# Inverse roots of the norms in the feed-forward part: ScalarE's square root against a guess and two iteration steps on VectorE

## The chip, the cores and the metric

One core of a Trainium2 chip runs one program. The metric is the device time of one execution in microseconds, the median over the runs shown. Lower is better. TensorE (PE), ScalarE (ACT), VectorE (DVE), GpSimd (POOL) and SyncE (SP) run their own instruction streams and meet through semaphores.

## The reference

One transformer layer with the norms behind the parts, on x of 2 x 2048 tokens by 256. What matters here are the three norms of each token, marked below, each with a mean, a variance and an inverse root.

```
z   = softmax(causal(q k^T / 8)) v              # 16 heads of 64
x1  = layernorm(x + z W_out + b_out)            # norm 1
h   = (x1 - mu) * rsqrt(var + 1e-5) * gamma + beta   # norm 2
u   = silu(h w1 + b1)                           # 1024 wide
out = layernorm(x1 + 0.5 * (u w2 + b2))         # norm 3
```

## The kernel before

**Attention** fills the first 1476 us and isn't touched. It leaves its outputs in DRAM, split in two float16 halves.

**Feed-forward part.** The 4096 tokens go in 8 blocks of 512 (`TOKB`, step i = 0 to 7, at most two blocks in flight), a block being 4 tiles of 128 tokens (`TPB`). Each engine has one function (`feed_forward_tensor`, `_scalar`, `_vector`, `_gpsimd`, `_sync`) and walks the steps in a fixed order, so the order of the work is the order written in these functions. Two blocks of out-projection and the first block's norms come ahead of step 0.

- PE, `step` (L1174): 11 turns of a loop over f. `fc1(i, f)` for f < 8 makes 128 of the 1024 columns (6 matmuls of 512 columns); `fc2(i, f-3)` follows three turns behind (12 matmuls of 256 columns); at f = 8 `turn(i+1)` (L1145) transposes the next block's normed rows, for which it waits on `norm_ready`. For i < 6 `out_projection(i+2)` (96 matmuls) ends the step.
- ACT, `step` (L1206): for each f a Silu out of PSUM into `a_full` (L1214) and two scaled Copies (L1218) into `a_hi` and `a_scaled`. Between them it takes the square roots of the norms, `root(n)` (L1202): the two of the next block behind f = 3 and f = 5, the one of norm 3 behind the step (that of step 6 behind f = 1 of step 7). In the trace an ACT_TABLE_LOAD stands ahead of a root that follows a Silu, and one ahead of the next Silu; `preload_silu` (L1230) takes the latter early.
- POOL (L1112): for each f one subtraction `a_lo = a_scaled - a_hi`, for which `fc2` waits (`a_split`).
- DVE, `step` (L1328): `to_norms(i+1)` (norms 1 and 2 of the next block, then `base`), `to_hT(i+1)` (scaled copies of the transposed rows out of PSUM, `hT_hi`, `hT` and `hT_lo`, for which the next step's `fc1` waits on `hT_ready`), then norm 3 of block i into `res`, which SP stores. `to_norms` starts when the block's out-projection is done (`wo_ready`).

A norm (`normalise`, L1256) is four BN_STATS, four BN_AGGR, an addition of EPS into `var_e` (L1265), a wait for ACT's root, a reciprocal (L1267) and four `tensor_scalar` (L1269) that subtract the mean and multiply by `rstd`. `Chain.done` lets each step of it raise a semaphore and waits for it on DVE itself.

Of the kernel before, what the change touches and what calls it, by code (L numbers as in the profile page):

```python
# [20 lines left out]
I32 = mybir.dt.int32  # L21
ALU = mybir.AluOpType
ACT = mybir.ActivationFunctionType
AX = mybir.AxisListType

P = 128
B, S, D = 2, 2048, 256
# [7 lines left out]
QB = 512  # L35
NQ = S // QB
NBLK = 2 * NQ
TPB = QB // P
# [3 lines left out]
START = 1  # L42
# [5 lines left out]
EPS = 1e-5  # L48
# [216 lines left out]
def program(nc, x, xT, wqkv, wout, b_out, gamma, beta, q1, s1, b1, q2, s2, b2, out, zT_dram):  # L265

    with ExitStack() as ctx:
        def sb(name, shape, dt=F32):
            return ctx.enter_context(nc.sbuf_tensor(name, shape, dt))

        def sem(name):
            return ctx.enter_context(nc.semaphore(name))
# [51 lines left out]
        def flat(t, dims, dt):  # L324
# [4 lines left out]
        w_hi_all, w_lo_all = flat(w_hi[:, :, :, :], 3, F32), flat(w_lo[:, :, :, :], 3, F32)  # L329
# [15 lines left out]
        y, ya, o = [w_hi_all[:, TPB * D * a:TPB * D * a + TPB * D].rearrange("p (t d) -> p t d", t=TPB) for a in range(3)]  # L345
        bo_s, b2_s, hb2 = [w_lo_all[:, D * a:D * a + D] for a in range(3)]
        a_scaled = w_lo_all[:, 3 * D:3 * D + 2 * QB].rearrange("p (d t) -> p d t", d=2)
        gam, bet, b1_s = sb("gam", [P, DT]), sb("bet", [P, DT]), sb("b1_s", [P, FT])
# [6 lines left out]
        res = qa_all[:, 0:SB].rearrange("p (k t d) -> p k t d", k=2, t=TPB)  # L355
# [6 lines left out]
        x1 = p_full_all[:, 4096:4096 + TPB * D].rearrange("p (t d) -> p t d", t=TPB)  # L362
        xn = p_parts_all[:, 4096:4096 + TPB * D].rearrange("p (t d) -> p t d", t=TPB)
        preload = sb("preload", [P, 1])
        stats, mv, var_e, std, rstd = (sb(n, d) for n, d in (("stats", [P, TPB, 6]), ("mv", [P, TPB, 2]),
                                                             ("var_e", [P, TPB]), ("std", [P, TPB]), ("rstd", [P, TPB])))
        WO, HT, FC, ZO = 0, 2, 4, 6

        passed = sem("passed")
# [24 lines left out]
        wo_ready, wo_read = sem("wo_ready"), sem("wo_read")  # L394
        first_norms, last_norm = sem("first_norms"), sem("last_norm")
        norm_ready, hT_ps, hT_parts, hT_ready = sem("norm_ready"), sem("hT_ps"), sem("hT_parts"), sem("hT_ready")
        var_ready, std_ready = sem("var_ready"), sem("std_ready")
        fc1_ready, act_ready, a_split = sem("fc1_ready"), sem("act_ready"), sem("a_split")
        fc2_used = sem("fc2_used")
        fc2_read = sem("fc2_read")  # L400
# [1 line left out]
        preloaded = sem("preloaded")  # L402
        silu_done, ffn_consts = sem("silu_done"), sem("ffn_consts")
        stored = [sem("stored0"), sem("stored1")]
# [3 lines left out]
        FIRST_PROJECTED = 0  # L408
        W_COLS = DF // W_PIECES
        SHIFT_ROWS = 6  # L410
        CONSTS = 13

        def reach(eng, semaphore, value):
# [129 lines left out]
        def attention_gpsimd(pool):  # L543
# [23 lines left out]
            for k, (dst, value) in enumerate(rows):  # L567
                if k:
                    pool.wait_ge(shift_rows, k)
                nc.gpsimd.memset(dst, value).then_inc(shift_rows, 1)  # L570
            pool.wait_ge(shift_rows, SHIFT_ROWS)

# [528 lines left out]
        def projects(i):  # L1101
            return FIRST_PROJECTED <= i < TOKB - 2
# [94 lines left out]
        def feed_forward_scalar(act):  # L1197
            act.sem_inc(act_ready, START)
            act.sem_inc(silu_done, START)
            act.sem_inc(preloaded, START)  # L1200

            def root(n):  # L1202
                act.wait_ge(var_ready, n + 1)
                nc.scalar.activation(std[:, :], var_e[:, :], ACT.Sqrt).then_inc(std_ready, 1)

            def step(i, k, more):  # L1206
                for f in range(FT):
                    act.wait_ge(fc1_ready, i * FT + f + 1 + START)

                    act.wait_ge(fc2_used, i * FT + START)  # L1210

                    act.wait_ge(a_split, i * FT + max(0, f - 1) + START)
                    at = i * FT + f + 1
                    nc.scalar.activation(a_full[:, f % 2, :], psum[:, FC + f % 2, :], ACT.Silu, bias=b1_s[:, f:f + 1],  # L1214
                                         scale=u_inverse[:, :]).then_inc(silu_done, 1)
                    act.wait_ge(silu_done, at + START)
                    for dst in (a_hi[:, f, :], a_scaled[:, f % 2, :]):
                        last = nc.scalar.activation(dst, a_full[:, f % 2, :], ACT.Copy, scale=a_scale[:, :])  # L1218
                    last.then_inc(act_ready, 1)
                    if f == 1 and i and not projects(i - 1):  # L1220
                        root(3 * i + 1)
                    if more and f in ROOTS_AT:
                        root(3 * i + 2 + ROOTS_AT.index(f))
                if not more:
                    root(3 * i + 2)
                elif projects(i):
                    root(3 * i + 4)
                    preload_silu(i + 1)

            def preload_silu(n):  # L1230


                act.wait_ge(preloaded, sum(projects(i) for i in range(n - 1)) + (n > 0) + START)
                nc.scalar.activation(preload[:, :], b1_s[:, 0:1], ACT.Silu).then_inc(preloaded, 1)

            ROOTS_AT = (3, 5)

            root(0)
            root(1)
            preload_silu(0)  # L1240
            over_blocks(act, step)

        def feed_forward_vector(dve):
# [9 lines left out]
                    instruction.then_inc(self.sem, 1)  # L1253
                    dve.wait_ge(self.sem, self.at)

            def normalise(chain, src, dst, n):  # L1256

                for t in range(TPB):
                    last = nc.vector.bn_stats(stats[:, t, :], src[:, t, :])
                chain.done(last)  # L1260
                dve.sem_inc(passed, 1)
                for t in range(TPB):
                    last = nc.vector.bn_aggr(mv[:, t, :], stats[:, t, :])
                chain.done(last)
                nc.vector.tensor_scalar(var_e[:, :], mv[:, :, 1], EPS, None, ALU.add).then_inc(var_ready, 1)  # L1265
                dve.wait_ge(std_ready, n + 1)
                chain.done(nc.vector.reciprocal(rstd[:, :], std[:, :]))  # L1267
                for t in range(TPB):
                    last = nc.vector.tensor_scalar(dst[:, t, :], src[:, t, :], mv[:, t, 0:1], rstd[:, t:t + 1],  # L1269
                                                   ALU.subtract, ALU.mult)  # L1270
                return last

            def constants():

# [18 lines left out]
                nc.vector.tensor_scalar(gam_s[:, :], gam[:, :], h_scale[:, :], None, ALU.mult)  # L1293
                step(nc.vector.tensor_scalar(bet_s[:, :], bet[:, :], h_scale[:, :], None, ALU.mult))

            NORMS, LAST = 9, 3

            def to_norms(i, k, n):
                chain = Chain(first_norms, i * NORMS)
                dve.wait_ge(wo_ready, i + 1)  # L1300
                dve.wait_ge(x_in[k], 16 * ((i - k) // 2 + 1) if isinstance(i, int) else (i - k) * 8 + 16)
                to = ZO if i == 1 else WO
                sums = psum[:, to:to + 2, :].rearrange("p k (t d) -> p (k t) d", t=2)
                b = i // NQ
                nc.vector.scalar_tensor_tensor(out=y[:, :, :], in0=sums, scalar=z_power[:, b:b + 1], in1=xs[:, k, :, :],
                                               op0=ALU.mult, op1=ALU.add).then_inc(wo_read, 1)
                dve.wait_ge(wo_read, i + 1 + START)
                chain.done(nc.vector.tensor_tensor(ya[:, :, :], y[:, :, :], bo_s.unsqueeze(1).to_broadcast([P, TPB, D]), ALU.add))
                chain.done(normalise(chain, ya, x1, n))

                last = normalise(chain, x1, xn, n + 1)
                last.then_inc(norm_ready, 1)
                nc.vector.scalar_tensor_tensor(out=base[:, k, :, :], in0=x1[:, :, :], scalar=2.0,
                                               in1=hb2.unsqueeze(1).to_broadcast([P, TPB, D]),
                                               op0=ALU.mult, op1=ALU.add).then_inc(first_norms, 1)
# [11 lines left out]

            def step(i, k, more):  # L1328
                if more:
                    to_norms(i + 1, 1 - k, 3 * i + 2)  # L1330
                    to_hT(i + 1)
                chain = Chain(last_norm, i * LAST)
                dve.wait_ge(fc2_used, i * FT + FT + START)
                dve.wait_ge(first_norms, i * NORMS + NORMS)

                dve.wait_ge(res_ready, i + START)
                sums = psum[:, ZO:ZO + 2, :].rearrange("p k (t d) -> p (k t) d", t=2)
                nc.vector.scalar_tensor_tensor(out=o[:, :, :], in0=sums, scalar=o_inverse[:, :], in1=base[:, k, :, :],
                                               op0=ALU.mult, op1=ALU.add).then_inc(fc2_read, 1)
                dve.wait_ge(fc2_read, i + 1 + START)  # L1340

                dve.wait_ge(stored[k], (((i - k) // 2) * 16 if isinstance(i, int) else (i - k) * 8) + START)
                last = normalise(chain, o, res[:, k, :, :], 3 * i + 4 if more else 3 * i + 2)
                last.then_inc(res_ready, 1)

            dve.wait_ge(biases_in, 16 * 2)
            nc.vector.tensor_scalar(hb2, b2_s, 0.5, None, ALU.mult).then_inc(b2_halved, 1)
            dve.wait_ge(b2_halved, 1)
            constants()
            to_norms(0, 0, 0)  # L1350
            to_hT(0)
            over_blocks(dve, step)

# [63 lines left out]
```

## Time and profile before

| | us |
|---|---|
| median of 3 runs (lowest to highest) | 1784.78 (1783.34 to 1786.6) |
| the profiled execution, its own time | 1787.09 |
| span of the profiled execution | 1785.2 |
| feed-forward part, from the first out-projection (1476.2) to the end | 309.0 |
| busy share of the span: PE, DVE, ACT, POOL | 95%, 78%, 88%, 76% |

How to read it: busy shares are of the whole span, most of which is attention. "Idle before" is the time an engine stood still ahead of an instruction, with the instruction that released it. Times of the trace are microseconds from the start of the span.

### The profile page before, as it was taken

How to read it: one execution, taken by the hardware profiler on the slowest of the kernel's cores; microseconds unless marked ns; L12 is line 12 of the kernel's file. 1: busy time of each engine (PE TensorE's matmuls, PEld its weight loads, DVE VectorE, ACT ScalarE, POOL GpSimd, SP SyncE). 2: the span in 40 equal slices, each digit the busy share in tenths (PEclk: the TensorE clock that was granted, in tenths of full speed). 3: DMA queues.
4: the chain of work that ended last, by engine and by line, in shares of the span. 5: the costliest groups of instructions: out<-in, count | busy, mean ns of one | idle time of the engine just before them, and what ended most of it. 6: DMA issues, size and time to landing. Idle time of an engine off the chain costs nothing.

```text
span 1785.2 us, 53985 instructions
## 1 busy us (share of the span) xinstructions
PE 1690.5 (95%) x21839; PEld 1152.2 (65%) x21839; DVE 1384.4 (78%) x3200; ACT 1562.2 (88%) x3243; POOL 1352.6 (76%) x833
## 2 busy tenths in 40 slices
PE   4799999999999999999999999999999998889986
PEld 2466666666666666666666666666666656666664
DVE  7978798978787878797989897989796845565554
ACT  4599999999999999999998999999999993765676
POOL 3498989898989898989898989888989891222223
PEclk9899999999999999999999999999999999999999
DMA  4003121211111111151212111111111502222300
GB/s 136 13 20 102 22 52 24 51 26 49 25 50 24 50 25 50 26 167 26 49 26 49 26 49 25 49 26 49 26 50 26 172 14 89 71 72 94 120 12 24
DMA packets 113207, 91.82 MB, mean 51 GB/s; under 512 B 73152, under 2 KB 100032, under 8 KB 111808
## 3 DMA queue, kind: packets, MB, share of 16 engines
q1 hardware_dynamic: 112960, 88.38, 18.3%
q8 instruction: 173, 2.83, 0.7%
q14 instruction: 74, 0.61, 0.1%
HBM read 33.82 MB, written 20.97 MB: 31 GB/s over the span
## 4 chain that ended last, share of the span: by engine, by line
PE 65%; ACT 21%; POOL 5%; DVE 4%; issue 4%; DMA 1%; SPq 0%; DVEq 0%; ACTq 0%
PE psum L1010 10%; PE psum L980 10%; PE psum L1014 10%; PE psum L951 7%; PE psum L1127 6%; PE psum L1038 5%; PE psum L1036 5%; PE psum L1040 5%; ACT p_parts L682 5%; ACT p_full L683 5%; PE psum L965 4%; POOL p_parts L578 4%; ACT kb L1214 2%; ACT w_lo L1218 2%; ACT p_full L1218 1%
## 5 line engine op out<-in xcount | busy, mean ns | idle before, releaser
L578 POOL TENSOR_TENSOR p_parts<-p_full,p_parts 128x1024 f16<-128x1024 f32 (+1 forms) x640 | 1161.1, 1841 | 196.4 <-ACT p_full L683 194.4
L682 ACT ACTIVATE p_parts<-psum 128x512 f16<-128x512 f32 (+3 forms) x1280 | 731.0, 571 | 60.6 <-PE psum L1014 35.2
L683 ACT ACTIVATE p_full<-psum 128x512 f32<-128x512 f32 (+3 forms) x1280 | 738.6, 579 | 0.0
L749 DVE TENSOR_REDUCE row_max<-psum 128x1 f32<-128x512 f32 x768 | 484.2, 681 | 16.1 <-PE psum L980 12.7
L1036 PE MATMUL psum<-v,p_parts 128*128 128x65 f16 x4352 | 487.2, 193 | 7.7 <-POOL p_parts L578 4.7
L1038 PE MATMUL psum<-v,p_parts 128*128 128x64 f16 x4352 | 488.7, 194 | 0.0
L1040 PE MATMUL psum<-v,p_parts 128*128 128x65 f16 x4352 | 486.2, 192 | 0.0
L1036 PEld LDWEIGHTS psum<-v,p_parts 128*128 128x128 f16 x4352 | 406.6, 97 | 83.7 <-POOL p_parts L578 12.5
L1010 PE MATMUL psum<-qa,ka 128*128 128x512 f16 (+3 forms) x1280 | 444.0, 348 | 4.0 <-ACT p_full L683 3.5
L1038 PEld LDWEIGHTS psum<-v,p_parts 128*128 128x128 f16 x4352 | 402.7, 97 | 69.6
L1014 PE MATMUL psum<-qb,kb 128*128 128x512 f16 (+3 forms) x1280 | 443.8, 347 | 3.0 <-DVE qb L762 2.9
L1040 PEld LDWEIGHTS psum<-v,p_parts 128*128 128x128 f16 x4352 | 404.2, 99 | 0.0
L980 PE MATMUL psum<-ka,qa 128*128 128x512 f16 (+3 forms) x1280 | 382.3, 347 | 11.0 <-DMA ka<-ka 2.4
L746 DVE CUSTOM_DVE_ANT_0 psum<-psum,mask_q 128x128 f32<-128x128 f32 (+3 forms) x512 | 238.2, 515 | 13.1 <-PE psum L980 11.3
L1118 POOL TENSOR_TENSOR p_parts<-w_lo,p_full 128x512 f16<-128x512 f32 x64 | 73.9, 1155 | 222.3 <-ACT w_lo L1218 222.3
L1010 PEld LDWEIGHTS psum<-qa,ka 128*128 128x128 f16 x1280 | 124.6, 97 | 75.9 <-ACT p_full L683 26.8
L1014 PEld LDWEIGHTS psum<-qb,kb 128*128 128x128 f16 x1280 | 124.9, 98 | 68.3 <-DVE qb L762 5.3
L980 PEld LDWEIGHTS psum<-ka,qa 128*128 128x128 f16 x1280 | 113.7, 97 | 80.7 <-DVE row_max L749 3.9
L775 DVE SCALAR_TENSOR_TENSOR qa<-psum,q_scale,qa 64x512 f16<-64x512 f32 x128 | 95.9, 749 | 67.8 <-ACT qa L668 66.8
L780 DVE TENSOR_TENSOR kb<-psum,ka 64x512 f16<-64x512 f32 x128 | 87.6, 684 | 46.6 <-ACT ka L671 45.7
L1016 PE MATMUL psum<-mask_k,ident_b 128*128 128x128 bf16 x512 | 111.6, 220 | 0.0
L1127 PE MATMUL psum<-ka,x_lo 128*128 128x512 f16 x384 | 93.1, 387 | 16.1 <-ACT kb L1214 11.7
(143 smaller groups left out, 2507.2 us busy)
## 6 DMA issues: line engine op xcount, KB each, us to landing
zT_dram<-z_T SPq DMA_DIRECT2D x16, 1024.0 KB, 4.7
qb<-qa SPq DMA_DIRECT2D x128, 64.0 KB, 1.9
ka<-ka SPq DMA_DIRECT2D x128, 64.0 KB, 1.9
shared_z<-zT_dram SPq DMA_DIRECT2D x4, 2048.0 KB, 8.4
x_hi<-zT_dram SPq DMA_DIRECT2D x4, 2048.0 KB, 9.4
shared_z<-xT_dram SPq DMA_DIRECT2D x8, 512.0 KB, 7.5
x_lo<-x_dram SPq DMA_DIRECT2D x8, 512.0 KB, 10.0
out_dram<-qa SPq DMA_DIRECT2D x8, 512.0 KB, 3.3
```

The lines of the kernel that those rows point to most:

```text
L578: nc.gpsimd.tensor_tensor(p_lo[:, at % NP, cols], p_full[:, at % NP, cols], p_hi[:, at % NP, cols], ALU.subtract).then_inc(probs_split, 1)
L682: nc.scalar.activation(p_hi[:, at % NP, to], lane_bank(a)[:, P * f:QB], ACT.Exp, scale=1.0 / SCORE)
L683: nc.scalar.activation(p_full[:, at % NP, to], lane_bank(a)[:, P * f:QB], ACT.Exp, scale=1.0 / SCORE).then_inc(lane_read, 1)
L746: nc.vector.tensor_tensor_reduce(out=bank, in0=bank, in1=mask_q[:, QB - w:QB], scale=1.0, scalar=NEG, op0=ALU.add, op1=ALU.max, accum_out= ...
L749: nc.vector.reduce_max(most, bank, AX.X).then_inc(ring_read, 1)
L980: last = nc.tensor.matmul(bank[:, 0:w], qa[:, h, P * tile:P * tile + P], ka[:, h, QB * c:QB * c + w], start=True, stop=True)
L1010: nc.tensor.matmul(to, ka[:, h, keys], qa[:, h, cols], start=True, stop=False)
L1014: last = nc.tensor.matmul(to, kb[:, h, keys], qb[:, h, cols], start=False, stop=k < TPB * q)
L1036: nc.tensor.matmul(z, p_hi[:, at % NP, cols], v[:, m % 2, k, h, 0:VZ], start=(k == 0 and t == 0), stop=False, skip_group_check=True)
L1038: nc.tensor.matmul(z[:, 0:C], p_hi[:, at % NP, cols], v[:, m % 2, k, h, V_LO:VS], start=False, stop=False, skip_group_check=True)
L1040: done = nc.tensor.matmul(z, p_lo[:, at % NP, cols], v[:, m % 2, k, h, 0:VZ], start=False, stop=last, skip_group_check=True)
L1127: mm = nc.tensor.matmul(psum_out, stationary[a], moving[b], start=first and n == 0, stop=last and n == 2, skip_group_check=True)
```

## The change

In the feed-forward part ACT takes no roots: `root` and its calls, the semaphores `var_ready` and `std_ready` and the repeated `preload_silu` go; one Silu at the start loads the table. DVE keeps the statistics and forms the inverse root in eight instructions on 128x4 elements, each chained to the one before by a semaphore: a guess out of the bits of `var_e` (one `tensor_scalar` on integers) and two iteration steps (`tensor_tensor` and `scalar_tensor_tensor`). One `dve.sem_inc(passed, 1)` behind BN_STATS goes as well. The small tiles lie in unused columns of `w_lo_all`, and norm 3 gets a mean and a root of its own. Nothing of the attention part, of PE, POOL and SP is changed.

```diff
-        stats, mv, var_e, std, rstd = (sb(n, d) for n, d in (("stats", [P, TPB, 6]), ("mv", [P, TPB, 2]),
-                                                             ("var_e", [P, TPB]), ("std", [P, TPB]), ("rstd", [P, TPB])))
+        small = w_lo_all[:, 3 * D + 2 * QB:3 * D + 2 * QB + 18 * TPB]
+        stats = small[:, 0:6 * TPB].rearrange("p (t s) -> p t s", t=TPB)
+        mvs = [small[:, (6 + 2 * a) * TPB:(8 + 2 * a) * TPB].rearrange("p (t s) -> p t s", t=TPB) for a in range(2)]
+        var_e, guess, near, part, ratio, bend = [small[:, a * TPB:a * TPB + TPB] for a in range(10, 16)]
+        rstds = [small[:, a * TPB:a * TPB + TPB] for a in range(16, 18)]
...
-            def root(n):
-                act.wait_ge(var_ready, n + 1)
-                nc.scalar.activation(std[:, :], var_e[:, :], ACT.Sqrt).then_inc(std_ready, 1)
...
-                    if f == 1 and i and not projects(i - 1):
-                        root(3 * i + 1)
-                    if more and f in ROOTS_AT:
-                        root(3 * i + 2 + ROOTS_AT.index(f))
-                if not more:
-                    root(3 * i + 2)
-                elif projects(i):
-                    root(3 * i + 4)
-                    preload_silu(i + 1)
...
-            root(0)
-            root(1)
-            preload_silu(0)
+            nc.scalar.activation(preload[:, :], b1_s[:, 0:1], ACT.Silu).then_inc(preloaded, 1)
+            act.wait_ge(preloaded, 1)
...
-            def normalise(chain, src, dst, n):
+            def spread(chain, src, mv, rstd):
                 for t in range(TPB):
                     last = nc.vector.bn_stats(stats[:, t, :], src[:, t, :])
                 chain.done(last)
-                dve.sem_inc(passed, 1)
                 for t in range(TPB):
                     last = nc.vector.bn_aggr(mv[:, t, :], stats[:, t, :])
                 chain.done(last)
-                nc.vector.tensor_scalar(var_e[:, :], mv[:, :, 1], EPS, None, ALU.add).then_inc(var_ready, 1)
-                dve.wait_ge(std_ready, n + 1)
-                chain.done(nc.vector.reciprocal(rstd[:, :], std[:, :]))
+                chain.done(nc.vector.tensor_scalar(var_e[:, :], mv[:, :, 1], EPS, None, ALU.add))
+                inverse_root(chain, var_e, rstd)
+
+            def inverse_root(chain, of, root):
+                chain.done(nc.vector.tensor_scalar(guess[:, :].bitcast(I32), of[:, :].bitcast(I32), -0.5, GUESS_BITS, ALU.mult, ALU.add))
+                chain.done(nc.vector.tensor_tensor(part[:, :], guess[:, :], of[:, :], ALU.mult))
+                chain.done(nc.vector.tensor_tensor(ratio[:, :], part[:, :], guess[:, :], ALU.mult))
+                chain.done(nc.vector.scalar_tensor_tensor(out=bend[:, :], in0=ratio[:, :], scalar=-10.0 / 3.0, in1=ratio[:, :],
+                                                          op0=ALU.add, op1=ALU.mult))
+                chain.done(nc.vector.scalar_tensor_tensor(out=near[:, :], in0=bend[:, :], scalar=5.0, in1=guess[:, :],
+                                                          op0=ALU.add, op1=ALU.mult))
+                chain.done(nc.vector.tensor_tensor(part[:, :], near[:, :], of[:, :], ALU.mult))
+                chain.done(nc.vector.scalar_tensor_tensor(out=ratio[:, :], in0=part[:, :], scalar=-0.5 * 0.375 ** 3, in1=near[:, :],
+                                                          op0=ALU.mult, op1=ALU.mult))
+                chain.done(nc.vector.scalar_tensor_tensor(out=root[:, :], in0=ratio[:, :], scalar=1.5 * 0.375, in1=near[:, :],
+                                                          op0=ALU.add, op1=ALU.mult))
```

## Rows read from the trace of the kernel before

**Rows 1.** Waits, 1470 to 1786 us: who waited for whom; us in total, times, longest

```profile
PE psum L1127 <- ACT kb L1214: 11.7, 15, 2.2
...
PE psum L1127 <- POOL p_parts L1118: 8.6, 14, 0.7
...
PE psum L1150 <- DVE p_parts L1269: 8.5, 8, 1.2
```

**Rows 2.** Timeline of PE, step 6: start us, us, instruction, count [idle before <-releaser]

```profile
1726.11 4.05 PE L1127 MATMUL psum<-ka,x_lo 128*128 128x512 f16 x18
...
1730.48 1.47 PE L1127 MATMUL psum<-ka,x_lo 128*128 128x512 f16 x6 [0.32 <-ACT kb L1214]
...
1731.79 0.38 PE L1127 MATMUL psum<-w_raw_rest,p_full 128*128 128x256 f16 x2
...
1733.10 1.46 PE L1127 MATMUL psum<-ka,x_lo 128*128 128x512 f16 x6
...
1739.54 1.47 PE L1127 MATMUL psum<-ka,x_lo 128*128 128x512 f16 x6 [1.07 <-ACT kb L1214]
...
1746.09 1.09 PE L1150 MATMUL psum<-ident,p_parts 128*128 128x128 f32 x8 [1.17 <-DVE p_parts L1269]
...
1747.02 0.38 PE L1127 MATMUL psum<-w_raw_rest,p_full 128*128 128x256 f16 x2
...
1752.53 4.05 PE L1127 MATMUL psum<-ka,x_lo 128*128 128x512 f16 x18
```

**Rows 3.** Timeline of step 2, ScalarE, GpSimd and VectorE

```profile
1580.01 0.78 ACT L1214 ACTIVATE kb<-psum,b_s,u_inverse 128x512 f32<-128x512 f32 x1 [6.57 <-PE psum L1127]
...
1582.06 0.76 ACT L1214 ACTIVATE kb<-psum,b_s,u_inverse 128x512 f32<-128x512 f32 x1
...
1582.23 1.16 POOL L1118 TENSOR_TENSOR p_parts<-w_lo,p_full 128x512 f16<-128x512 f32 x1 [15.58 <-ACT w_lo L1218]
...
1583.25 0.17 DVE L1265 TENSOR_SCALAR var_e<-mv 128x4 f32<-128x4 f32 x1
...
1591.11 0.78 ACT L1214 ACTIVATE kb<-psum,b_s,u_inverse 128x512 f32<-128x512 f32 x1
```

**Rows 4.** Timeline of PE: starts of step 0, step 2 and the wait in step 7

```profile
1503.07 7.74 PE L1127 MATMUL psum<-ka,x_lo 128*128 128x512 f16 x24 [4.36 <-issue]
...
1510.64 0.38 PE L1127 MATMUL psum<-w_raw_rest,p_full 128*128 128x256 f16 x2
...
1578.51 4.05 PE L1127 MATMUL psum<-ka,x_lo 128*128 128x512 f16 x18
...
1761.88 1.47 PE L1127 MATMUL psum<-ka,x_lo 128*128 128x512 f16 x6 [2.20 <-ACT kb L1214]
```

**Rows 5.** Timeline of VectorE: to_hT's subtraction ahead of step 0; copies and subtraction in step 6

```profile
1501.74 1.23 DVE L1326 TENSOR_TENSOR ka<-kb,ka 128x1024 f16<-128x1024 f32 x1
...
1747.23 1.53 DVE L1322 TENSOR_SCALAR ka<-psum,gam_s,bet_s 128x512 f16<-128x512 f32 x2
...
1750.23 2.00 DVE L1326 TENSOR_TENSOR ka<-kb,ka 128x1024 f16<-128x1024 f32 x1
```

**Rows 6.** Timeline of VectorE: the last norm, at the end

```profile
1777.76 1.40 DVE L1259 BATCH_NORM_STATS2 stats<-w_hi 128x6 f32<-128x256 f32 x4
...
1779.72 0.17 DVE L1265 TENSOR_SCALAR var_e<-mv 128x4 f32<-128x4 f32 x1
...
1780.38 1.38 DVE L1269 TENSOR_SCALAR qa<-w_hi,mv,rstd 128x256 f32<-128x256 f32 x4
```

**Rows 7.** Timelines of GpSimd and VectorE: two places where they meet

```profile
1477.25 1.15 POOL L584 TENSOR_TENSOR z_parts<-z_pair,z_parts 128x512 f16<-128x512 f32 x1 [2.16 <-ACT z_parts L690]
...
1477.68 0.73 DVE L1287 SCALAR_TENSOR_TENSOR a_bound<-u_inverse,a_bound 128x1 f32<-128x1 f32 x1
...
1593.34 1.16 POOL L1118 TENSOR_TENSOR p_parts<-w_lo,p_full 128x512 f16<-128x512 f32 x1 [3.83 <-ACT w_lo L1218]
...
1593.42 1.10 DVE L1265 TENSOR_SCALAR var_e<-mv 128x4 f32<-128x4 f32 x1
```

More of the change, by code:

```diff
@@ L396, in program @@
         norm_ready, hT_ps, hT_parts, hT_ready = sem("norm_ready"), sem("hT_ps"), sem("hT_parts"), sem("hT_ready")
-        var_ready, std_ready = sem("var_ready"), sem("std_ready")
         fc1_ready, act_ready, a_split = sem("fc1_ready"), sem("act_ready"), sem("a_split")
@@ L410, in program @@
         SHIFT_ROWS = 6
+        GUESS_BITS = float(0x5f3759df)
         CONSTS = 13
@@ L1199, in feed_forward_scalar @@
             act.sem_inc(silu_done, START)
-            act.sem_inc(preloaded, START)
-            def root(n):
-                act.wait_ge(var_ready, n + 1)
-                nc.scalar.activation(std[:, :], var_e[:, :], ACT.Sqrt).then_inc(std_ready, 1)
             def step(i, k, more):
@@ L1219, in step @@
                     last.then_inc(act_ready, 1)
-                    if f == 1 and i and not projects(i - 1):
-                        root(3 * i + 1)
-                    if more and f in ROOTS_AT:
-                        root(3 * i + 2 + ROOTS_AT.index(f))
-                if not more:
-                    root(3 * i + 2)
-                elif projects(i):
-                    root(3 * i + 4)
-                    preload_silu(i + 1)
[L1230 to L1236, printed above, removed]
-            root(0)
-            root(1)
-            preload_silu(0)
+            nc.scalar.activation(preload[:, :], b1_s[:, 0:1], ACT.Silu).then_inc(preloaded, 1)
+            act.wait_ge(preloaded, 1)
             over_blocks(act, step)
@@ L1264, in normalise, with rescale @@
                 chain.done(last)
-                nc.vector.tensor_scalar(var_e[:, :], mv[:, :, 1], EPS, None, ALU.add).then_inc(var_ready, 1)
-                dve.wait_ge(std_ready, n + 1)
-                chain.done(nc.vector.reciprocal(rstd[:, :], std[:, :]))
+                chain.done(nc.vector.tensor_scalar(var_e[:, :], mv[:, :, 1], EPS, None, ALU.add))
[13 more added lines that the diff above has]
+                                                          op0=ALU.add, op1=ALU.mult))
+            def rescale(src, dst, mv, rstd):
                 for t in range(TPB):
@@ L1271, in normalise @@
                 return last
+            def normalise(chain, src, dst):
+                spread(chain, src, mvs[0], rstds[0])
+                return rescale(src, dst, mvs[0], rstds[0])
             def constants():
@@ L1294, in constants, with to_norms @@
                 step(nc.vector.tensor_scalar(bet_s[:, :], bet[:, :], h_scale[:, :], None, ALU.mult))
-            NORMS, LAST = 9, 3
-            def to_norms(i, k, n):
+            SPREAD = 11
+            NORMS, LAST = 2 * SPREAD + 3, SPREAD
+            def to_norms(i, k):
                 chain = Chain(first_norms, i * NORMS)
@@ L1308, in to_norms @@
                 chain.done(nc.vector.tensor_tensor(ya[:, :, :], y[:, :, :], bo_s.unsqueeze(1).to_broadcast([P, TPB, D]), ALU.add))
-                chain.done(normalise(chain, ya, x1, n))
-                last = normalise(chain, x1, xn, n + 1)
+                chain.done(normalise(chain, ya, x1))
+                last = normalise(chain, x1, xn)
                 last.then_inc(norm_ready, 1)
@@ L1329, in step @@
                 if more:
-                    to_norms(i + 1, 1 - k, 3 * i + 2)
+                    to_norms(i + 1, 1 - k)
                     to_hT(i + 1)
@@ L1340, in step @@
                 dve.wait_ge(fc2_read, i + 1 + START)
-                dve.wait_ge(stored[k], (((i - k) // 2) * 16 if isinstance(i, int) else (i - k) * 8) + START)
-                last = normalise(chain, o, res[:, k, :, :], 3 * i + 4 if more else 3 * i + 2)
+                dve.wait_ge(stored[k], ((i - k) // 2) * 16 + START)
+                spread(chain, o, mvs[1], rstds[1])
+                last = rescale(o, res[:, k, :, :], mvs[1], rstds[1])
                 last.then_inc(res_ready, 1)
@@ L1349, in feed_forward_vector @@
             constants()
-            to_norms(0, 0, 0)
+            to_norms(0, 0)
             to_hT(0)
```

## The prediction

> **What bounds the kernel now.** The change touches nothing ahead of 1476 us, so I read the waits of the feed-forward part alone, then the timeline of PE through one block, then what ScalarE, GpSimd and VectorE did beside it.
>
> VectorE's own waits for ScalarE's roots cost nothing as long as nobody waits for VectorE, so the waits to read are PE's [rows 1]: 11.7 us for Silu, 8.6 us for GpSimd's subtraction, 8.5 us for VectorE's normed rows.
>
> The timeline of one block [rows 2] gives PE's prices. One fc1 issues in 1.31 us (1730.48 to 1731.79), one fc2 in 1.31 (to 1733.10), a pair in about 2.61 when nothing is late (several pairs; the one shown takes 2.62), the turn in 0.93 (1746.09 to 1747.02). The start, from the first fc1 to the first fc2, takes 5.68 (1726.11 to 1731.79). Against these prices PE loses in the block:
> - 1739.54 - (1733.10 + 2 x 2.61) = 1.22 ahead of an fc1, for Silu;
> - 1746.09 - (1739.54 + 2 x 2.61) = 1.33 ahead of the turn, for the norms;
> - 1752.53 - 1747.02 - 3 x 1.31 = 1.58 between the last fc2s, for GpSimd, which is late because ScalarE is.
>
> Sum 4.13 us. All of it hangs on ScalarE. Its cadence for one f is 2.05 us [rows 3], less than PE's 2.61, so without roots ScalarE is never last. But the Silu due at 1582.06 + 3 x 2.04 = 1588.18 starts at 1591.11: a root with a table load ahead and one behind puts it 2.93 us back, twice in a block. The block's period is (1726.11 - 1578.51) / 4 = 36.90 [rows 2, 4]; the floor by PE's own work is 36.90 - 4.13 = 32.77.
>
> **The change, part by part.**
>
> *ScalarE without roots, steps 1 to 5:* the three losses go, 5 x 4.13 = 20.65 us, if nothing else is late. GpSimd's first subtraction ends at 1582.23 + 1.16, 4.88 after the step's start of 1578.51 [rows 3, 4]; it is wanted at 5.68, and later ones are earlier still against their fc2.
>
> *Step 0* starts at 1503.07 and takes 7.57 to its first fc2 (1510.64) [rows 4], slower than the 5.68 elsewhere; I keep that. Before, it lasted to 1578.51 - 36.90 = 1541.61, so 38.54. After: 7.57 + (32.77 - 5.68) = 34.66. Gain 3.88.
>
> *Step 6* has no out-projection behind it, so hT_ready is next in line. VectorE's copies start 1.14 after the turn's start and the subtraction 3.00 later (1747.23, 1750.23) [rows 2, 5]. That one took 2.00, with GpSimd running, and 1.23 ahead of step 0 (1501.74), with GpSimd idle; GpSimd will be done by then, so I take 1.23, with 2.00 as the other end. hT_ready is then some 5.4 to 6.2 after the turn's start, while PE gets there in 0.93 + 3.93 = 4.86. A new gap of 0.6 (to 1.4): gain 3.53.
>
> *Step 7:* the first fc2 ended at 1752.53 + 5.68 + 1.31 = 1759.52, the next fc1 started at 1761.88 [rows 2, 4]; the 2.36 were step 6's last root. Gain 2.36.
>
> *Eight small instructions for a norm.* From var_e to the rescaling took 0.66 (1779.72 to 1780.38) [rows 6] for three links: var_e, ScalarE's root, the reciprocal; 0.22 a link. var_e itself lasts 0.17. A link of the new chain lies between 0.17 and 0.22; I take 0.21. Nine links are 1.89, so a norm gets 1.23 longer where ScalarE was ready. That counts where VectorE is the path: norms 1 and 2 of block 0 ahead of step 0 (+2.46) and the last norm (+1.23). GpSimd is idle at both places. The removed sem_inc may give back something, at most one link (0.2) for each of these three norms; I take nothing and keep 0.6 for the range.
>
> Sum so far: 2.46 - 3.88 - 20.65 - 3.53 - 2.36 + 1.23 = **-26.7 us**.
>
> *Cover of the other norms.* In a step, norms 1 and 2 are covered if they end before the turn is due, which is now 5.68 + 4 x 2.61 + 1.31 = 17.43 after the start S. VectorE reaches var_e at S + 4.74 (1583.25) [rows 3, 4]; then 1.89, rescaling 1.41, statistics of norm 2 1.96 (1777.76 to 1779.72) [rows 6], 1.89, 1.41: S + 13.3. Slack 4.1.
>
> But VectorE is seen stopped by GpSimd [rows 7]. A `scalar_tensor_tensor` on one column took 0.73 and ended when GpSimd's subtraction did (1477.68 + 0.73 against 1477.25 + 1.15). The `tensor_scalar` var_e took 1.10 in place of 0.17 and ended with GpSimd's run as well (1593.42 + 1.10 against 1593.34 + 1.16). So seven of the eight small instructions, of the first kind or with the same two inputs, wait out a GpSimd run in which they would start; and I take it that the guess and the rescaling, `tensor_scalar` from SBUF to SBUF like var_e, do too. No row shows a rescaling beside GpSimd, so this is the open bound. The Trainium skill (SBUF — State Buffer, Who interferes with whom) has this as one rule: a VectorE instruction with two SBUF inputs, or a `tensor_scalar` in a 2-port mode, can't run while a GpSimd instruction that reads SBUF does. By it the sum is the one with the delay below, -22.8; without it, -26.7; the trace [rows 7] agrees with it for both kinds, no row shows the rescaling.
>
> GpSimd's runs of 1.16 will start at S + 3.72, then about 2.04 apart: 5.8, 7.8, 9.9, 11.9, 13.9, 16.0. Walking VectorE through them: a small instruction meets the run of 5.8 (resumes at 7.0), the rescaling that of 7.8 (9.2), var_e of norm 2 that of 11.9 (13.1), a small one that of 13.9 (15.2), the rescaling that of 16.0 (17.3). Five hits of about 1 us: the norms end at S + 18.0, and the turn starts some 0.65 late. Steps 1 to 6 pay this, 6 x 0.65 = +3.9; step 0 has 1.9 us more room. If the rescaling isn't stopped, the norms end at about 15.2 and the term is 0. GpSimd held up by VectorE in turn costs nothing: `base` at S + 18, some 1.2 us like the subtraction of the same 1024 elements [rows 5], may push its last run to end at 20.4, wanted after 21.
>
> **Sum: -26.7 + 3.9 = -22.8 us.** Against the profiled execution's span of 1785.2 that is 1762.4, or 1764.3 for its own time of 1787.09. The median of the runs is 2.3 below that time: 1784.78 - 22.8 = **1762.0**.
>
> **The rivals.**
> - *The norms stay covered* (the rescaling isn't stopped, or the links are shorter): PE has only its own work, -26.7, 1758.1. For it: 2.8 us of the five hits hang on the rescaling. Against: var_e is its kind. 0.30.
> - *One more GpSimd run is lost in each block,* since the phases of the two engines decide and I know them to some 0.2 us: 6 x 1.16 = +7.0, 1769.0. 0.10.
> - *Slower: VectorE's chain becomes the bound.* If a small link costs e more than 0.21, 24e come on top at start and end, and in steps 1 to 6 16e - 4.1: -26.7 + 24e + 6 (16e - 4.1) is zero at e = 0.43. From 0.64 us a link the kernel is slower; at the 0.77 that the one column beside GpSimd took, it loses 16 us, 1800.7. Against: that instruction was late only while GpSimd ran, and var_e takes 0.17 alone. 0.02.
> - *The change doesn't take the loads away* because Copy and Silu need two tables: then ScalarE stays as late and the chains are extra, +3.7, 1788.5. Against: Silu follows two Copies at a cadence of 2.05 now, with no room for a load. 0.01.
> - Something between, so that the gain is within the noise: 0.02.
>
> The forecast itself gets 0.55.
>
> **How the numbers follow.** A measurement of this kernel can tell 0.2%, 3.6 us, from no change. The forecast and the first two rivals are all beyond that: 0.95 faster. 0.02 for within 0.2%, 0.03 for slower, from the last three rivals. The range goes from the first rival less the sem_inc and the spread of the runs (1758.1 - 0.6 - 1.4 = 1756.1) to the second (1769.0).
>
> **What would show it.** No ACT_TABLE_LOAD in the blocks, a period of 33.4 (32.8 if the norms are covered) in place of 36.90, no wait of PE for Silu but some 0.4 near the start of a step, none for GpSimd, and one of about 0.65 ahead of the turn; in step 6 some 0.6 for hT_ready. Step 0 starts at 1505.5. Small instructions of 0.17 to 0.2 us, two of eight near 1.1 where GpSimd runs, and a rescaling of near 1 us among the four. The forecast is wrong if the rescalings keep 0.41 beside GpSimd, if the turn is late by more than 1 us, or if a small link takes over 0.3 with GpSimd idle.

## The result and the profile after

The changed kernel takes 1758.5 us (median of 4 runs, 1756.55 to 1759.43) against 1785.69 for the kernel before (4 runs, the three shown ahead and one more). The ratio is 0.9846, 95% interval 0.9829 to 0.9863: 27.2 us, 1.5%, faster. The profiled execution has a span of 1757.1 us, 28.1 less than before.

| busy us of the span | PE | DVE | ACT | POOL |
|---|---|---|---|---|
| before | 1690.5 | 1384.4 | 1562.2 | 1352.6 |
| after | 1684.1 | 1433.2 | 1496.4 | 1356.1 |

ScalarE got 65.8 us less to do and VectorE 48.8 us more. Neither number says what the change is worth; the waits of PE do. Here are those that are left of them in the feed-forward part (the view of the waits, 1470 to 1760 us; who waited for whom, us in total, times, longest). They answer to [rows 1]:

```profile
PE psum L1130 <- issue: 4.4, 1, 4.4
...
PE psum L1153 <- DVE p_parts L1266: 2.3, 1, 2.3
...
PE psum L1130 <- ACT kb L1212: 2.2, 7, 0.3
...
PE psum L1130 <- DVE ka L1329: 0.4, 1, 0.4
```

The 11.7 us for Silu are 2.2, seven times the 0.3 us near the start of a step, and the 8.6 us for GpSimd are gone. Of the 8.5 us for the normed rows 2.3 are left, once, ahead of step 0. New is 0.4 us for hT_ready, once, at the start of step 7. The 4.4 us under issue stand ahead of step 0, before and after alike. PE's timeline shows the blocks (start us, us, instruction, count, idle before); it answers to [rows 2, 4]:

```profile
1486.89 10.64 PE L1130 MATMUL psum<-shared_w,x_hi 128*128 128x256 f16 x96
...
1505.34 7.15 PE L1130 MATMUL psum<-ka,x_lo 128*128 128x512 f16 x24 [4.37 <-issue]
...
1539.34 4.05 PE L1130 MATMUL psum<-ka,x_lo 128*128 128x512 f16 x18
...
1556.74 1.08 PE L1153 MATMUL psum<-ident,p_parts 128*128 128x128 f32 x8
...
1702.97 4.05 PE L1130 MATMUL psum<-ka,x_lo 128*128 128x512 f16 x18
...
1725.77 4.06 PE L1130 MATMUL psum<-ka,x_lo 128*128 128x512 f16 x18 [0.40 <-DVE ka L1329]
```

A block takes (1702.97 - 1539.34) / 5 = 32.73 us, where it took 36.90. The turn starts at 1556.74, 17.40 after the start of its step, and has no idle time in front of it. So the norms are covered, but look at VectorE and GpSimd in the same step:

```profile
1539.54 1.28 DVE L1308 SCALAR_TENSOR_TENSOR w_hi<-psum,z_power,x_lo 128x1024 f32<-128x1024 f32 x1 [3.93 <-PE psum L1130]
...
1544.68 0.16 DVE L1252 TENSOR_TENSOR w_lo<-w_lo 128x4 f32<-128x4 f32 x1
...
1545.28 1.01 DVE L1257 TENSOR_TENSOR w_lo<-w_lo 128x4 f32<-128x4 f32 x1
...
1546.71 2.22 DVE L1266 TENSOR_SCALAR p_full<-w_hi,w_lo 128x256 f32<-128x256 f32 x4
...
1551.24 1.14 DVE L1251 TENSOR_TENSOR w_lo<-w_lo 128x4 f32<-128x4 f32 x1
...
1553.39 1.02 DVE L1260 SCALAR_TENSOR_TENSOR w_lo<-w_lo 128x4 f32<-128x4 f32 x1
...
1554.45 2.23 DVE L1266 TENSOR_SCALAR p_parts<-p_full,w_lo 128x256 f32<-128x256 f32 x4
...
1545.10 1.17 POOL L1121 TENSOR_TENSOR p_parts<-w_lo,p_full 128x512 f16<-128x512 f32 x1 [0.88 <-ACT w_lo L1216]
...
1547.13 1.34 POOL L1121 TENSOR_TENSOR p_parts<-w_lo,p_full 128x512 f16<-128x512 f32 x1 [0.87 <-ACT w_lo L1216]
...
1555.27 1.25 POOL L1121 TENSOR_TENSOR p_parts<-w_lo,p_full 128x512 f16<-128x512 f32 x1 [0.88 <-ACT w_lo L1216]
```

An undisturbed link takes 0.16 us (1544.68). Three of the sixteen take 1.01 to 1.14, each because GpSimd's subtraction runs, and each group of four rescalings 2.22 or 2.23 in place of 1.38 [rows 6]. The last one ends at 1554.45 + 2.23 = 1556.68, which is 0.06 us before the turn starts; in steps 2 to 6 it is 0.07 or 0.08. Norms 1 and 2 fit in front of the turn with nothing to spare. VectorE as a whole isn't full: it still stands idle for 3.93 us in a block, waiting for the out-projection (the first line above), so it is the order of the work and not its amount that is at the limit.

The last norm, at the end, answers to [rows 6]:

```profile
1747.31 1.28 DVE L1341 SCALAR_TENSOR_TENSOR w_hi<-psum,o_inverse,qb 128x1024 f32<-128x1024 f32 x1 [13.50 <-PE psum L1130]
...
1750.48 0.17 DVE L1244 TENSOR_SCALAR w_lo<-w_lo 128x4 f32<-128x4 f32 x1
...
1752.27 1.39 DVE L1266 TENSOR_SCALAR qa<-w_hi,w_lo 128x256 f32<-128x256 f32 x4
```

From var_e to the rescaling it takes 1.79 us where it took 0.66, nine links of 0.20.

### The profile page after: what moved, and what is told of

Read it like the earlier page. It is cut to its first block, busy times and chain, and to the rows that moved or that the text cites. A ratio compares the mean times of both kernels' runs of the same rounds, so it can differ in the third digit from the quotient of the medians.

```text
span 1757.1 us, 54055 instructions
## 1 busy us (share of the span) xinstructions
PE 1684.1 (96%) x21839; PEld 1153.6 (66%) x21839; DVE 1433.2 (82%) x3368; ACT 1496.4 (85%) x3169; POOL 1356.1 (77%) x833
## 4 chain that ended last, share of the span: by engine, by line
PE 73%; ACT 14%; issue 4%; DVE 4%; POOL 3%; DMA 1%; SPq 1%; DVEq 0%; ACTq 0%
PE psum L1130 12%; PE psum L1013 10%; PE psum L983 10%; PE psum L1017 10%; PE psum L954 7%; PE psum L1041 6%; PE psum L1039 6%; PE psum L1043 5%; ACT p_parts L685 5%; ACT p_full L686 5%; PE psum L968 4%; POOL p_parts L581 2%; PE psum L1019 1%; ACT qa L671 1%; DMA ka<-ka 1%
## 5 line engine op out<-in xcount | busy, mean ns | idle before, releaser
L1212 ACT ACTIVATE kb<-psum,b_s,u_inverse 128x512 f32<-128x512 f32 x64 | 49.0, 766 | 133.3 <-PE psum L1130 104.0
```

## The experiments

Two things were to be tested. The first is what made the kernel before slow: the table loads (theory A), or the hand-over of each root between VectorE and ScalarE (theory B). The second is what the new chain costs: on the path at start and end only, with no room left in the blocks, or otherwise.

A profile's whole span also holds the attention part, which differs by some us from run to run, and the first out-projection, which took from 10.6 to 13.1 us in these profiles. So beside each run's time stands the stretch from the start of the second out-projection (1486.89 in the rows of after above) to the end of the span, and the period of a block.

| kernel | median us (runs) | ratio to before, 95% | stretch us | period us |
|---|---|---|---|---|
| before | 1785.69 (4) | 1 | 298.5 | 36.90 |
| changed | 1758.5 (4) | 0.9846 (0.9829 to 0.9863) | 270.2 | 32.73 |
| e8 changed, again | 1760.11 (5) | 0.9846 (0.9832 to 0.986) | 270.0 | 32.71 |
| e1 loads only | 1792.43 (8) | 1.0027 (1.0015 to 1.0039) | 303.2 | 36.87 to 37.81 |
| e2 Copy for Sqrt | 1756.47 (4) | 0.9826 (0.9807 to 0.9845) | 267.7 | 32.68 |
| e3 hybrid | 1755.97 (4) | 0.9824 (0.9808 to 0.9841) | 267.9 | 32.71 |
| e9 hybrid, again | 1757.0 (4) | 0.9827 (0.981 to 0.9844) | 266.9 | 32.71 |
| e4 sem_inc back | 1760.97 (2) | 0.9853 (0.983 to 0.9876) | 270.9 | 32.71 or 32.94 |
| e5 GpSimd sliver | 1761.18 (4) | 0.9855 (0.9833 to 0.9877) | 270.3 | 32.69 |
| e6 root twice | 1804.59 (3) | 1.0084 (1.0059 to 1.011) | 315.6 | 38.2 to 39.8 |
| e7 one step | 1754.68 (4) | 0.9815 (0.9793 to 0.9837) | 268.8 | 32.68 |

### e1: the table loads alone

```diff
                     last.then_inc(act_ready, 1)
+                    if more and f in (3, 5):
+                        nc.scalar.activation(spare[:, :], b1_s[:, 0:1], ACT.Sqrt, scale=0.0)
```

> The changed kernel with one idle square root on ScalarE behind f = 3 and one behind f = 5 of steps 0 to 6, which nobody waits for: the table loads are back, the hand-over of roots is not. Theory A (the loads held the kernel up, by making Silu and with it GpSimd's subtraction late): the block's period goes from 32.73 back to 36.90, steps 0 to 6 give back nearly all they gained, 3.9 + 5 x 4.13 + 3.7 = 28 us, so a span near 1785. Theory B (VectorE's and the turn's wait for ScalarE's root was what cost): nobody waits for these roots, so the period stays near 32.8, the span near 1757.

Measured: 1792.43 us, all that the change had gained and 5 us more; the span of the profile, 1791.7, is 7 us above theory A's 1785. ScalarE and PE in step 1:

```profile
1554.92 1.28 ACT L1220 ACT_TABLE_LOAD   x1
...
1556.42 1.28 ACT L1213 ACT_TABLE_LOAD   x1
...
1557.72 0.78 ACT L1213 ACTIVATE kb<-psum,b_s,u_inverse 128x512 f32<-128x512 f32 x1
...
1558.55 1.47 PE L1131 MATMUL psum<-ka,x_lo 128*128 128x512 f16 x6 [1.04 <-ACT kb L1213]
...
1563.77 1.04 PE L1154 MATMUL psum<-ident,p_parts 128*128 128x128 f32 x8
...
1568.15 0.39 PE L1131 MATMUL psum<-w_raw_rest,p_full 128*128 128x256 f16 x2 [2.03 <-POOL p_parts L1122]
...
1572.44 7.80 PE L1131 MATMUL psum<-shared_w,x_hi 128*128 128x256 f16 x70
...
1582.92 4.05 PE L1131 MATMUL psum<-ka,x_lo 128*128 128x512 f16 x18
```

Nobody waits for these roots, and the turn (1563.77) isn't late. Still the block takes 1582.92 - 1545.16 = 37.76, since PE waits 1.04 for Silu and 2.03 for GpSimd's subtraction, and then some more for the next one. In the kernel before, the wait ahead of the turn had taken a part of the time that PE would else have stood waiting for GpSimd: 1.33 + 1.58 there, nearly the same here without the 1.33. The run of GpSimd that PE waits for ends 22.93 us after the start of the step (1566.93 + 1.16 - 1545.16), in the kernel before 23.00. The three waits of [rows 2] weren't three losses, but one delay of ScalarE by 2 x 2.9 us, seen at three places. Theory A holds for the cause; the wait of the turn for the norms was worth nothing by itself.

The expectation of 1785 left two things out: e1 keeps the longer norms at start and end, some 3 us, and PE's clock. The clock is the surplus over 36.9 in four of steps 1 to 5 (granted clock by windows of step 1; us, PE busy, PEclk, DMA share, GB/s):

```profile
1568.00:1570.00 2.00, 1.85 (x11) 0.63 0.00 0
...
1570.00:1572.00 2.00, 2.00 (x11) 0.51 0.00 0
...
1572.00:1574.00 2.00, 2.00 (x21) 1.00 0.00 0
```

After the 2.03 us without work the clock falls to its lower level, 1.2 GHz, and the two fc2s behind the wait take 1572.44 - 1568.15 = 4.29. In steps 0 and 3 they take 3.41 and the clock doesn't fall, after a wait of 2.02, as long as the waits of steps 4 and 6, where it does.

### e2: the hand-over alone

```diff
-                nc.scalar.activation(std[:, :], var_e[:, :], ACT.Sqrt).then_inc(std_ready, 1)
+                nc.scalar.activation(std[:, :], var_e[:, :], ACT.Copy).then_inc(std_ready, 1)
```

> The kernel before with ScalarE's Sqrt replaced by a Copy of the same four columns, which needs no table load; the inverse root is left out of the result. Hand-over, order and waits stay as before. Theory A (loads): no loads, so the period falls to 32.75 as in the changed kernel; and since the short hand-over of 0.66 us stays at the start and at the end, where the changed kernel pays 1.1 us more for each of three norms, it ends some 3.3 us below the changed kernel, at a span near 1754. Theory B (hand-over): the period stays well above 32.8 and the gain is at most half, a span of 1770 or more.

Measured: 1756.47 us, period 32.68, stretch 267.7. The whole gain is there with the hand-over as it was, and 2.5 us on top in the stretch, where theory A had 3.3. So the loads are the cause from both sides: they alone bring the time back (e1), and without them nothing else of the old scheme costs (e2).

### e3 and e9: ScalarE keeps the three roots where it stands idle

The two norms ahead of step 0 and the last one take ScalarE's root; the table loads lie where ScalarE has nothing to do.

```diff
+            root(0)
+            root(1)
             nc.scalar.activation(preload[:, :], b1_s[:, 0:1], ACT.Silu).then_inc(preloaded, 1)
...
             over_blocks(act, step)
+            root(2)
...
-                chain.done(nc.vector.tensor_scalar(var_e[:, :], mv[:, :, 1], EPS, None, ALU.add))
-                inverse_root(chain, var_e, rstd)
+                var = nc.vector.tensor_scalar(var_e[:, :], mv[:, :, 1], EPS, None, ALU.add)
+                if root is None:
+                    chain.done(var)
+                    inverse_root(chain, var_e, rstd)
+                    return
+                var.then_inc(var_ready, 1)
+                dve.wait_ge(std_ready, root + 1)
+                chain.done(nc.vector.reciprocal(rstd[:, :], std[:, :]))
```

> The changed kernel, but the two norms ahead of step 0 and the last norm take their root from ScalarE as before, where it stands idle and the table loads are hidden; all others on VectorE. Theory A (the new chain costs only at these three places, 1.79 - 0.66 = 1.1 us for each norm): 3.3 us less than the changed kernel, minus what a load behind the last Copy may leave uncovered (nothing, since PE still has over 3 us of fc2 to do then): a span near 1753.7, ratio to before 0.983. Theory B (these places are covered too, or the clock at the start of step 0 gives the time back): within 1 us of the changed kernel's 1757.1.

> The kernel in which ScalarE keeps the three roots where it stands idle, once more beside the changed kernel. Theory A (the new chain costs 1.1 us for each of three norms, and the clock at the start of step 0 takes back 0.9): 2.4 us below the changed kernel of this call. Theory B (the difference of 2.5 us between the two medians is the spread of the first out-projection, which took between 10.6 and 13.1 us in the profiles): no difference beyond 1 us.

> The changed kernel once more, unchanged, beside the next one on the same chip, to compare the two: 1757 to 1760, 26 to 29 us below the kernel before. Theory A and theory B say the same.

Measured: 1755.97 us, and beside the changed kernel on the same chip 1757.0 against 1760.11. The medians lie 2.5 and 3.1 us below, the stretches 2.3 and 3.1. The intervals of the ratios still overlap, so the sign rests on both pairs and on the traces together. VectorE and ScalarE at the end of e3:

```profile
1748.80 0.17 DVE L1253 TENSOR_SCALAR w_lo<-w_lo 128x4 f32<-128x4 f32 x1
...
1749.57 1.38 DVE L1283 TENSOR_SCALAR qa<-w_hi,w_lo 128x256 f32<-128x256 f32 x4
...
1742.55 1.28 ACT L1223 ACT_TABLE_LOAD   x1
...
1749.00 0.20 ACT L1223 ACTIVATE std<-w_lo 128x4 f32<-128x4 f32 x1 [5.17 <-DVE w_lo L1253]
```

var_e to the rescaling takes 0.77 in place of 1.79; the load (1742.55) is over five us before the root is wanted. At the other end, step 0 starts 2.0 us earlier after the second out-projection (1502.89 - 1486.48 = 16.41, changed kernel 1505.34 - 1486.89 = 18.45). Of the 3.1 us saved at the two ends step 0 took 0.9 back in e3, but not in e9, which is the same kernel. The first 24 matmuls of step 0 in e3 and in e9:

```profile
1502.89 8.03 PE L1132 MATMUL psum<-ka,x_lo 128*128 128x512 f16 x24 [4.36 <-issue]
...
1499.36 7.03 PE L1132 MATMUL psum<-ka,x_lo 128*128 128x512 f16 x24 [4.37 <-issue]
```

In the changed kernel they take 7.15 us, in e8 7.14. The granted clock is 0.50 for 5.5 us of that time in e3 and for 3.4 us in e9, though PE does the same work ahead of them. So theory A has the price of the new chain right, about 1 us for each of three norms; the 0.9 that the clock was to take back belongs to a single profile. e3 has the lowest median of the kernels here that compute the whole result.

### e4: the removed sem_inc put back

```diff
                 chain.done(last)
+                dve.sem_inc(passed, 1)
                 for t in range(TPB):
                     last = nc.vector.bn_aggr(mv[:, t, :], stats[:, t, :])
```

> The changed kernel with the one removed sem_inc(passed) on VectorE put back behind BN_STATS of each norm. Theory A (in steps 1 to 6 the norms end 0.06 us before the turn is due, and the sem_inc is worth the 0.11 us between BN_STATS and BN_AGGR that the kernel before shows more): the turn waits 0.1 to 0.2 us in six steps, and three norms on the path get 0.11 longer: 0.9 to 1.5 us more, a span near 1758.3, and a wait of PE ahead of the turn shows in each step. Theory B (the norms have more room than that, since the GpSimd run that stops them absorbs a shift): only the 0.33 us of start and end, no wait ahead of the turn.

Measured: 1760.97 us in two runs, a stretch 0.7 us longer. VectorE's second rescaling and PE's turn in steps 1 and 2:

```profile
1552.94 1.10 DVE L1251 TENSOR_SCALAR w_lo<-w_lo 128x4 int32<-128x4 int32 x1
...
1556.30 2.25 DVE L1267 TENSOR_SCALAR p_parts<-p_full,w_lo 128x256 f32<-128x256 f32 x4
...
1585.95 1.02 DVE L1252 TENSOR_TENSOR w_lo<-w_lo 128x4 f32<-128x4 f32 x1
...
1589.04 2.22 DVE L1267 TENSOR_SCALAR p_parts<-p_full,w_lo 128x256 f32<-128x256 f32 x4
...
1541.01 4.05 PE L1130 MATMUL psum<-ka,x_lo 128*128 128x512 f16 x18
...
1558.61 1.10 PE L1153 MATMUL psum<-ident,p_parts 128*128 128x128 f32 x8
...
1573.95 4.05 PE L1130 MATMUL psum<-ka,x_lo 128*128 128x512 f16 x18
...
1591.35 1.06 PE L1153 MATMUL psum<-ident,p_parts 128*128 128x128 f32 x8
```

Both theories hold in part. In step 1 the turn starts 17.60 after the step, 0.20 late, and in step 2 at 17.40, in time; of steps 1 to 5 two are late and three aren't. In step 2 the run of GpSimd stops the instruction behind the guess (1585.95), as in the changed kernel: the shift of 2 x 0.11 us only moves it inside the run, the end of the run decides, and the shift is swallowed. In step 1 the guess itself starts inside the run and is stopped in its place (1552.94), so one link more is left to do behind the run: the 0.20. The guess takes 1.10 us there: the `tensor_scalar` on int32 is stopped like the others.

### e5: GpSimd's runs cut short

```diff
-                    nc.gpsimd.tensor_tensor(a_lo[:, f, :], a_scaled[:, f % 2, :], a_hi[:, f, :], ALU.subtract).then_inc(a_split, 1)
+                    nc.gpsimd.tensor_tensor(a_lo[:, f, 0:1], a_scaled[:, f % 2, 0:1], a_hi[:, f, 0:1], ALU.subtract).then_inc(a_split, 1)
```

> The changed kernel with GpSimd's subtraction cut to one of its 512 columns; the low halves of the activations are left out of the result. Nothing else is shortened. Theory A (GpSimd's runs stop VectorE's small instructions and rescalings, but the norms are covered all the same): every link takes 0.16 to 0.17 us and every rescaling 0.41, the norms of steps 1 to 6 end near 12.8 us after the step's start in place of 17.34, and the time stays, a span of 1756 to 1758, period 32.73. Theory B (the collisions cost time now): the period falls below 32.7 and the span by 2 us or more.

Measured: a period of 32.69 and a stretch of 270.3, the changed kernel's; the median, 1761.18, is higher, but the interval of its ratio holds the changed kernel's 0.9846. A group of rescalings and one of links (us busy, mean ns of one; first the changed kernel, then this one, whose view begins later, at 1500 us, and so has fewer of them):

```profile
L1266 DVE TENSOR_SCALAR p_full<-w_hi,w_lo 128x256 f32<-128x256 f32 x32 | 17.0, 595 | 0.3
...
L1251 DVE TENSOR_TENSOR w_lo<-w_lo 128x4 f32<-128x4 f32 x24 | 9.8, 408 | 0.8
```

```profile
L1266 DVE TENSOR_SCALAR p_full<-w_hi,w_lo 128x256 f32<-128x256 f32 x28 | 9.7, 408 | 0.3
...
L1251 DVE TENSOR_TENSOR w_lo<-w_lo 128x4 f32<-128x4 f32 x23 | 3.7, 163 | 0.8
...
1555.49 1.38 DVE L1266 TENSOR_SCALAR p_parts<-p_full,w_lo 128x256 f32<-128x256 f32 x4
```

The rescaling falls from 595 to 408 ns and the link from 408 to 163. The norms now end at 1555.49 + 1.38 = 1556.87, which is 12.85 after the start of the step (1544.02). They are 4.5 us earlier, the turn still starts 17.40 after the step, and the time is the same. So the collisions of a block cost norms 1 and 2 4.5 us, and the kernel nothing.

### e6: the inverse root twice

```diff
                 inverse_root(chain, var_e, rstd)
+                inverse_root(chain, var_e, rstd)
```

> The changed kernel with the eight instructions of the inverse root done twice for each norm (same result). Theory A (no room: the norms end 0.06 us before the turn is due): 16 links more are 3.15 us, with GpSimd's runs between them 4 to 6 us, and the turn is late by that in steps 1 to 6, by a little less in step 0; with 3 x 1.6 us at start and end 30 to 45 us more, slower than the kernel before or equal to it, a span of 1787 to 1802. Theory B (room of some 4 us, as the chain would have with GpSimd idle): only start and end, 4.7 us more, a span of 1762.

Measured: 1804.59 us, span 1803.0, slower than the kernel before. PE in step 1 and its granted clock (us, PE busy, PEclk, DMA share, GB/s):

```profile
1546.19 4.05 PE L1130 MATMUL psum<-ka,x_lo 128*128 128x512 f16 x18
...
1567.75 1.97 PE L1153 MATMUL psum<-ident,p_parts 128*128 128x128 f32 x8 [3.99 <-DVE p_parts L1267]
```

```profile
1567.00:1570.00 3.00, 2.25 (x11) 0.50 0.02 5
```

The turn starts 21.56 after the step, 4.16 late, and ahead of step 0 PE's turn waits 5.50 in place of 2.35, that is 16 links of 0.197. Theory A. The span came out 1 us above the range. The expectation had left out PE's clock: after 3.99 us of idle time the clock falls to 1.2 GHz, the turn takes 1.97 in place of 1.08, and the fc2s behind it are slow too. A block takes up to 39.8 us.

### e7: one iteration step less

```diff
-                chain.done(nc.vector.scalar_tensor_tensor(out=near[:, :], in0=bend[:, :], scalar=5.0, in1=guess[:, :],
+                chain.done(nc.vector.scalar_tensor_tensor(out=root[:, :], in0=bend[:, :], scalar=5.0, in1=guess[:, :],
                                                           op0=ALU.add, op1=ALU.mult))
-                chain.done(nc.vector.tensor_tensor(part[:, :], near[:, :], of[:, :], ALU.mult))
-                chain.done(nc.vector.scalar_tensor_tensor(out=ratio[:, :], in0=part[:, :], scalar=-0.5 * 0.375 ** 3, in1=near[:, :],
-                                                          op0=ALU.mult, op1=ALU.mult))
-                chain.done(nc.vector.scalar_tensor_tensor(out=root[:, :], in0=ratio[:, :], scalar=1.5 * 0.375, in1=near[:, :],
-                                                          op0=ALU.add, op1=ALU.mult))
```

> The changed kernel without the second iteration step (three links fewer for each norm; the second step and its constant factor are left out of the result). Theory A (covered in the steps, on the path at start and end): 3 x 0.6 = 1.8 us less, of which the lower clock at the start of step 0 takes back up to 0.5, period 32.7 as before, a span near 1755.5. Theory B (the length of the chain still sets the period): the period falls too and the gain is over 3 us.

Measured: 1754.68 us, a period of 32.68, a stretch of 268.8, 1.4 less than the changed kernel's. Theory A, with 1.8 us less for the chains and 0.7 more at the start of step 0, whose first 24 matmuls take 7.85 us against 7.15 in this profile (e3 and e9 show how much that differs by itself). The span of its profile, 1757.2, isn't lower than the changed kernel's, since its first out-projection took 12.31 us.

## Why the prediction was right, and where it was not

The time, 1758.5 us, lies in the range and 3.5 below the forecast of 1762.0. It is the first rival, "the norms stay covered", with its 1758.1. That this number fits to 0.4 us is in part luck: its terms add up to -26.7 where the profiles show -28.3, and the same kernel had a median of 1760.11 in e8. The wait of 0.65 us ahead of the turn and the period of 33.4 that the forecast asked for didn't come. By the prediction's own steps:

| term | predicted us | measured us |
|---|---|---|
| norms 1 and 2 ahead of step 0 | +2.46 | +2.05 |
| step 0 | -3.88 | -4.54 |
| steps 1 to 5 | -20.65 | -20.87 |
| step 6 | -3.53 | -3.62 |
| step 7 | -2.36 | -2.37 |
| last norm | +1.23 | +1.02 |
| sum without the turn | -26.7 | -28.3 |
| the turn late by VectorE and GpSimd | +3.9 | 0 |

Each measured term is the difference between two stretches of the two profiles. From the second out-projection to step 0: (1505.34 - 1486.89) - (1503.07 - 1486.67), the last of these times being the start of that out-projection before. Step 0: 1539.34 - 1505.34 = 34.00 against 38.54. Steps 1 to 5: 163.63 against 184.50. Step 6: 1725.77 - 1702.97 = 22.80 against 26.42. Step 7: from its start to the first VectorE instruction behind it, 1747.31 - 1725.77 = 21.54 against 23.91. Last norm: from there to the rescaling, 4.96 against 3.94. The attention part ended 0.2 us later, which gives the 28.1 of the spans.

- **The floor by PE's own work** was right to 0.04 us a block (32.77 against 32.73), and so was the claim that all of PE's losses hang on ScalarE's table loads; e1 and e2 show it from both sides.
- **The step that failed is the turn's delay of 0.65 us.** The mechanism was right: VectorE's small instructions, var_e and the rescalings are all stopped by GpSimd's runs, in the order that the walk gave but for the second norm's var_e (the chain came to that run a little earlier, and its third link was stopped in its place). The sizes were off. The walk ended at 18.0 us and VectorE at 17.34. The link was taken at 0.21 and is 0.197 (18 x 0.013 = 0.23 us), the sem_inc was taken at nothing and was worth 0.11 in each of the two norms (0.22), and the collisions took 4.5 us (e5) where the walk had 18.0 - 13.3 = 4.7. These three add up to the 0.66, but they don't act one by one, since the collisions swallow small shifts. Since the turn is due at 17.40, the term is zero, by 0.06 us: with the sem_inc back (e4) the turn is late in two of steps 1 to 5.
- **The rival that came true had two reasons, and the one that weighed most in its 0.30 fell.** It was to hold if "the rescaling isn't stopped, or the links are shorter". The rescaling is stopped (2.22 against 1.38 us, and 1.38 again in e5), as the prediction took it by likeness to var_e and as the Trainium skill (SBUF — State Buffer, Who interferes with whom) states. That leaves its other reason, the shorter links, together with the removed sem_inc, which the rival doesn't name. Neither is shown to be enough by itself, and e4 shows that the sem_inc isn't needed in four of steps 1 to 6. That this rival came true was close, and in so far luck.
- **Step 0** gained 0.66 more than predicted. I had kept its slow start of 7.57 us as it was; it took 6.99 (1512.33 for the first fc2). PE's first 24 matmuls took 7.15 in place of 7.74 us. PE begins 2.3 us later than before, and less of its work falls into the stretch at the lower clock (0.50 from 1505 to 1507 us in both profiles, full from 1509 on in both). That the later start is the reason isn't shown. With the long norms ahead the 24 matmuls take 7.14 to 7.49 us (changed kernel, e8, e1, e5), with the short ones 7.74 (before), 7.97 (e2) and 8.03 (e3), but 7.03 in e9. The 0.66 may be chance, and to take the start as it was in one profile was too sure.
- **"GpSimd held up by VectorE costs nothing"** held for the changed kernel, whose GpSimd runs were stretched to 1.34 and 1.25 us by the rescaling. It holds in e1 too, though PE waits 2.03 for GpSimd there: the run that it waits for takes its usual 1.16 us and is late because ScalarE is.
- **The slower rival** put the point of decision at a link of 0.64 us. e6, with two chains of 0.2, which is much like one with a link of 0.4, is already slower than before by 0.8%. The rule was off because it counted a longer chain at its own length, and neither the GpSimd runs that it meets on its way nor the clock that falls while PE waits.

## What to carry to other kernels

Where an engine switches tables inside a loop, look for the delay at every place behind it in the pipeline and count it once: three waits of PE for three engines were one delay of ScalarE, and with the wait for VectorE taken away its time moved into the next one (e1). When work goes to another engine, compute when it ends against the instant it is wanted, with the collisions, and not from shares of busy time; here 48.8 us more on VectorE cost 3 us, and twice the chain cost 45 more (e6). Keep the old way where it was free: in this kernel the roots at start and end are about 1 us cheaper each on the engine that stands idle (e3, e9). And don't take a start at the lower clock from one profile as a constant: it took between 7.03 and 8.03 us in two profiles of one kernel.

## What was not expected of the hardware

- A collision goes both ways, as the Trainium skill (SBUF — State Buffer, Who interferes with whom) says; the trace agrees. With `base` on VectorE first (1522.28, 1.21 us), GpSimd's subtraction that starts 0.31 us later takes 1.92 us in place of 1.16:

```profile
1522.59 1.92 POOL L1121 TENSOR_TENSOR p_parts<-w_lo,p_full 128x512 f16<-128x512 f32 x1 [0.71 <-ACT w_lo L1216]
...
1522.28 1.21 DVE L1316 SCALAR_TENSOR_TENSOR qb<-p_full,w_lo 128x1024 f32<-128x1024 f32 x1
```

- A wait of about two microseconds in the middle of dense work is at times enough for PE's clock to fall to 1.2 GHz: of the seven waits of 2.02 or 2.03 us in steps 0 to 6 of e1 it fell behind five and not behind those of steps 0 and 3, though the steps are otherwise alike. It cost 0.9 us each time it fell. Why it differs wasn't found.
- Two instruction streams that stop each other absorb small shifts: 0.22 us more of work in e4 moved the end of the norms by 0 in three steps and by 0.2 in two.
